# A convolution and score kernel: third products one pair late at the end, low parts on GpSimd, channel 62 averaged on TensorE, last output in four pieces

## The reference

```python
# layer 0: a long convolution per channel, by FFT of twice the size; k is the outer product of two filters
k = einsum('ijk,imk->ijmk', hx, hy)[0]                 # hx, hy: small sine networks times a decay
z = irfft2(rfft2(x) * rfft2(k) / 512)[..., :256, :256] + x * bias
# layer 1, per channel, all 4 images
scores = einsum('bpsd,bptd->bpst', z, z) / sqrt(256)
red = sum(scores * weights[None], axis=-1, keepdims=True)
y = z + red
out = (y - mean(y)) * rsqrt(var(y) + 1e-5) * gamma + beta   # mean and var over images, rows and columns
```

## Time and profile before

| what | value |
|---|---|
| median of 3 runs | 959.41 us (957.51, 959.53, 959.41) |
| profiled execution, own time | 957.47 us |
| its span, first to last instruction | 955.0 us |
| PE busy | 932.5 us, 98% |
| DVE, ACT, GpSimd busy | 751.8, 682.0, 668.0 us |
| mean granted clock of PE | 0.990 |

### The profile page before, as it was taken

How to read it: one execution, slowest core, us unless ns; L and a number is a source line. 1 busy time by engine, 2 the same in 40 slices (tenths; PEclk the granted TensorE clock), 3 DMA queues, 4 the chain that set the end, 5 groups by cost and what they waited for, 6 DMA issues and landing times.

```text
span 955.0 us, 18894 instructions
## 1 busy us (share of the span) xinstructions
PE 932.5 (98%) x5308; PEld 816.1 (85%) x5308; DVE 751.8 (79%) x2460; ACT 682.0 (71%) x1088; POOL 668.0 (70%) x518
## 2 busy tenths in 40 slices
PE   7999999999999999999999999999999999999993
PEld 5888888888888888888888888888888888888882
DVE  2677887887887888878878878878788788788785
ACT  2447777777777777777777777777777777777756
POOL 2676776777777767767767767777777677677650
PEclk9999999999999999999999999999999999999996
DMA  7767998888899998888798999988898899888735
GB/s 224 262 177 214 252 259 293 266 239 289 241 266 297 233 292 278 287 233 273 243 276 283 223 303 272 290 260 246 258 274 267 291 211 304 289 274 244 245 121 182
DMA packets 91439, 244.23 MB, mean 256 GB/s; under 512 B 17312, under 2 KB 42272, under 8 KB 83232
## 3 DMA queue, kind: packets, MB, share of 16 engines
q1 hardware_dynamic: 73280, 235.73, 82.5%
q10 hardware_dynamic: 18144, 8.33, 3.5%
HBM read 176.65 MB, written 67.37 MB: 256 GB/s over the span
## 4 chain that ended last, share of the span: by engine, by line
PE 95%; issue 2%; DVE 1%; DMA 1%; POOL 1%; ACT 0%; POOLq 0%; DVEq 0%
PE ps_c L507 36%; PE ps_u L507 31%; PE ps_z L507 27%; DMA toep_whole<-filters_padded 1%; DVE z_sb L680 0%; DMA par<-params_in 0%; POOL zl L402 0%; DVE products L702 0%; DMA filters_padded<-z_sb 0%; DVE z_sb L786 0%; DVE z_sb L614 0%; POOL toep L376 0%; DVE ul L729 0%; POOL rstd L364 0%; ACT zh L491 0%
## 5 line engine op out<-in xcount | busy, mean ns | idle before, releaser
L402 POOL TENSOR_TENSOR zl<-z_sb,zh 128x1024 fp32r<-128x1024 f32 x126 | 301.5, 2393 | 237.3 <-ACT zh L491 237.3
L702 DVE CUSTOM_DVE_ANT_0 products<-z_sb,ps_c 128x256 bf16<-128x256 f32 x508 | 183.7, 418 | 155.2 <-PE ps_c L507 155.2
L507 PE MATMUL ps_z<-uh,toep 128*128 128x512 f32 x768 | 271.4, 408 | 0.1
L469 ACT ACTIVATE out_sb<-z_sb,shift,gain 128x256 f32<-128x256 f32 x496 | 257.2, 591 | 11.6 <-DMA out<-out_sb 6.1
L448 ACT ACTIVATE uh<-ps_u 128x1024 fp32r<-128x1024 f32 x127 | 130.5, 1027 | 177.7 <-PE ps_u L507 177.7
L507 PE MATMUL ps_u<-toep,xh 128*128 128x256 f32 x1016 | 235.5, 313 | 2.8 <-POOL toep L376 2.7
L507 PE MATMUL ps_c<-zh,wh 128*128 128x512 f32 x508 | 197.8, 389 | 1.2 <-DVE zl L691 0.7
L507 PE MATMUL ps_c<-zh,wl 128*128 128x512 f32 x508 | 197.7, 389 | 0.0
L507 PE MATMUL ps_c<-zl,wh 128*128 128x512 f32 x508 | 197.7, 389 | 0.0
L507 PE MATMUL ps_u<-toep_whole,xt_sb 128*128 128x128 f32 x1016 | 196.0, 274 | 0.0
L713 DVE BATCH_NORM_STATS2 stat<-z_sb 128x6 f32<-128x256 f32 x512 | 179.4, 413 | 0.0
(11 more groups left out here) (72 smaller groups left out, 907.0 us busy)
## 6 DMA issues: line engine op xcount, KB each, us to landing
xt_sb<-xt_in SPq DMA_DIRECT2D x64, 1024.0 KB, 10.3
x_sb<-x_in SPq DMA_DIRECT2D x128, 512.0 KB, 8.4
out<-out_sb SPq DMA_DIRECT2D x124, 512.0 KB, 6.8
w_sb<-wt_in SPq DMA_DIRECT2D x64, 256.0 KB, 7.2
toep_whole<-filters_padded SPq DMA_DIRECT2D x64, 256.0 KB, 7.4
everyone<-partition_moments ACTq DMA_DIRECT2D x63, 128.0 KB, 8.8
out<-z_sb SPq DMA_DIRECT2D x4, 512.0 KB, 2.8
partition_moments<-own ACTq DMA_DIRECT2D x63, 1.0 KB, 5.7
```

Of the source, the lines that this page charges most:

```text
L402: nc.gpsimd.tensor_tensor(zl[:, zs.slot(2)], z_sb[:, r, h], zh[:, zs.slot(2)].bitcast(F32), ALU.subtract)\
L469: last = nc.scalar.activation(to[:, k, b], z_sb[:, r, h, k, b], ACT.Identity, bias=shift[:, r, g:g + 1], scale=gain[:, r])
L507: return nc.tensor.matmul(o, a, b, start=start, stop=stop)
L702: last = nc.vector.tensor_tensor_reduce(products[:, cs.slot(2), k, b], z_sb[:, r, h, k, b], bank[:, k, b], 1.0 / math.sqrt(SIDE), 0.0, ALU ...
```

## The change

- In steps 128 and 129 PE runs only third product 124, one half (output block) in each; 125, 126 and 127 come in the ending, in `ps_u`, `ps_c`, `ps_u`. DVE sums 124 in step 129.
- `zl` of pairs 126 and 127 is computed by GpSimd. `zh` and `zl` of pair 127 lie in slot 0 of `uh` and `ul` and wait for second product 126 instead of an earlier third product.
- Channel 62's moments are no longer sent through DRAM but averaged by PE, as channel 63's are, between and behind the halves of third product 127. `ps_avg` and `last_moment` get a place for each of the two channels.
- GpSimd's power for channel 61 and shift for channel 62 move behind its `zl(127)`; DVE's ending is reordered.
- Channel 63 is stored in four pieces of 256 KB, each as soon as its block is normed; ACT's two instructions are both in the second half.

```diff
         return st.static() and PAIRS - count <= st.number() < PAIRS
+    def last_pair(st):
+        return st.static() and st.number() == PAIRS - 1
...
+        last_moment = sb("last_moment", [P, 2, 1])
+        ps_avg = ps("ps_avg", [P, 2, 3])
...
             return par[:, bass.ds(st.channel(COL_CHAN + kind * CH), 1)]
+        def z_parts(zs):
+            if last_pair(zs):
+                return uh[:, 0], ul[:, 0]
+            return zh[:, zs.slot(2)], zl[:, zs.slot(2)]
...
                     if ending(done, 2):
-                        sp.wait_ge(last_done, done.number() - (PAIRS - 2) + 1)
-                        sp.wait_ge(last_done_act, done.number() - (PAIRS - 2) + 1)
+                        for k in range(BLOCKS):
+                            sp.wait_ge(last_done, BLOCKS * h + k + 1)
+                            if h == 1:
+                                sp.wait_ge(last_done_act, k + 1)
+                            sp.dma_start(out[m, :, h, k, :, :].rearrange("p b w -> p (b w)"),
+                                         normed[:, k].rearrange("p b w -> p (b w)"))\
+                                .then_inc(stored[h], 16)
...
             for h in range(2):
-                sp.wait_ge(stored[h], 16 * CH)
+                sp.wait_ge(stored[h], 16 * (CH - 1 + BLOCKS))
...
                 ms = st.trail(LAG_MEAN)
-                if starts(ms):
+                if starts(ms) and not ending(ms, 4):
...
                 vs = st.trail(LAG_POWER)
-                if starts(vs) and not ending(vs, 4):
+                if starts(vs) and not ending(vs, 6):
...
                 zs = st.trail(LAG_Z)
-                if active(zs) and not ending(zs, 2):
+                if active(zs):
...
                     r, h = zs.ring(XR), zs.half()
-                    nc.gpsimd.tensor_tensor(zl[:, zs.slot(2)], z_sb[:, r, h],
-                                            zh[:, zs.slot(2)].bitcast(F32), ALU.subtract)\
+                    high, low = z_parts(zs)
+                    nc.gpsimd.tensor_tensor(low, z_sb[:, r, h], high.bitcast(F32), ALU.subtract)\
...
             run_steps(pool, PAIRS, 2 * UNROLL, LAG_MEAN - 3, stage)
+            inverse_deviation(Step(0, PAIRS - 6))
+            shift_means(Step(0, PAIRS - 4))
...
                 ms = st.trail(LAG_MEAN)
-                if starts(ms) and not ending(ms, 2):
+                if starts(ms) and not ending(ms, 4):
...
                 ss = st.trail(LAG_SPREAD)
-                if starts(ss) and not ending(ss, 2):
+                if starts(ss) and not ending(ss, 4):
...
                     wait(act, z_ready, zs, 1)
-                    wait(act, c_done, zs, -1)
+                    if last_pair(zs):
+                        wait(act, y_done, zs, 0)
+                    else:
+                        wait(act, c_done, zs, -1)
                     r, h = zs.ring(XR), zs.half()
-                    nc.scalar.activation(zh[:, zs.slot(2)], z_sb[:, r, h],
-                                         ACT.Copy).then_inc(zh_ready, 1)
+                    nc.scalar.activation(z_parts(zs)[0], z_sb[:, r, h], ACT.Copy).then_inc(zh_ready, 1)
...
             act.wait_ge(last_shift, 1)
-            for i in range(PAIRS - 2, PAIRS):
-                r, h = i // 2 % XR, i % 2
-                rows = z_sb[:, r, h, BLOCKS - 1, PAIR - 1]
-                g = (h * BLOCKS + BLOCKS - 1) * PAIR + PAIR - 1
+            r = (CH - 1) % XR
+            for k in range(BLOCKS):
+                rows = z_sb[:, r, 1, k, PAIR - 1]
+                g = (BLOCKS + k) * PAIR + PAIR - 1
...
                 last.then_inc(y_done, 1)
-            def product_c(cs, bank):
+            def product_c(cs, bank, blocks=range(BLOCKS)):
...
                 wait(pe, zl_ready, cs, 1)
-                s, w = cs.slot(2), cs.ring(2)
-                for a in range(BLOCKS):
+                w = cs.ring(2)
+                high, low = z_parts(cs)
+                for a in blocks:
...
                         w_h, w_l = wh[:, w, k, P * a:P * (a + 1)], wl[:, w, k, P * a:P * (a + 1)]
-                        mm(bank[:, a], w_h, zh[:, s, k], k == 0, False)
-                        mm(bank[:, a], w_h, zl[:, s, k], False, False)
-                        last = mm(bank[:, a], w_l, zh[:, s, k], False, k == BLOCKS - 1)
-                last.then_inc(c_done, 1)
+                        mm(bank[:, a], w_h, high[:, k], k == 0, False)
+                        mm(bank[:, a], w_h, low[:, k], False, False)
+                        last = mm(bank[:, a], w_l, high[:, k], False, k == BLOCKS - 1)
+                if BLOCKS - 1 in blocks:
+                    last.then_inc(c_done, 1)
...
                 cs = st.trail(LAG_RED)
-                if active(cs):
+                if st.static() and st.number() >= PAIRS:
+                    late = Step(0, PAIRS - 4)
+                    wait(pe, red_ready, late, 0)
+                    product_c(late, ps_c, [st.number() - PAIRS])
+                elif active(cs):
...
             run_steps(pe, PAIRS, UNROLL, END_STEPS, stage)
-            end = [Step(0, i) for i in range(PAIRS - 2, PAIRS)]
-            product_y(end[1])
+            end = [Step(0, i) for i in range(PAIRS - 3, PAIRS)]
+            def average_first(m):
+                pe.wait_ge(mean_in, m + 1)
+                mm(ps_avg[:, m % 2, 0:2], ones[:, :].bitcast(F32), own[:, m % XR], True, True).then_inc(averaged, 1)
+            def average_moment(m):
+                pe.wait_ge(moment_in, m - (CH - 2) + 1)
+                mm(ps_avg[:, m % 2, 2:3], ones[:, :].bitcast(F32), last_moment[:, m % 2], True, True)\
+                    .then_inc(averaged, 1)
+            product_y(end[2])
+            product_c(end[0], ps_u)
+            pe.wait_ge(red_ready, PAIRS - 3)
+            product_c(end[1], ps_c)
             pe.wait_ge(red_ready, PAIRS - 2)
-            product_c(end[0], ps_c)
-            product_c(end[1], ps_u)
-            pe.wait_ge(mean_in, CH)
-            mm(ps_avg[:, 0:2], ones[:, :].bitcast(F32), own[:, (CH - 1) % XR], True, True).then_inc(averaged, 1)
-            pe.wait_ge(moment_in, 1)
-            mm(ps_avg[:, 2:3], ones[:, :].bitcast(F32), last_moment[:, :], True, True).then_inc(averaged, 1)
+            product_c(end[2], ps_u, [0])
+            average_first(CH - 2)
+            product_c(end[2], ps_u, [1])
+            average_moment(CH - 2)
+            average_first(CH - 1)
+            average_moment(CH - 1)
...
                     op0=ALU.mult, op1=ALU.add).then_inc(z_ready, 1)
-            def low_z(zs):
-                nc.vector.tensor_tensor(zl[:, zs.slot(2)], z_sb[:, zs.ring(XR), zs.half()],
-                                        zh[:, zs.slot(2)].bitcast(F32), ALU.subtract)\
-                    .then_inc(zl_ready, 1)
...
                 cs = st.trail(LAG_RED)
-                if active(cs):
+                if st.static() and st.number() >= PAIRS:
+                    if st.number() == PAIRS + 1:
+                        gain_and_offset(Step(0, PAIRS - 8))
+                        reduce_rows(Step(0, PAIRS - 4), ps_c)
+                elif active(cs):
...
             run_steps(dve, PAIRS, 2 * UNROLL, END_STEPS, stage)
-            end = [Step(0, i) for i in range(PAIRS - 2, PAIRS)]
+            end = [Step(0, i) for i in range(PAIRS - 3, PAIRS)]
             before, final = Step(0, PAIRS - 4), Step(0, PAIRS - 2)
-            low_z(end[0])
-            whole_z(end[1])
+            def first_averages(vs):
+                r, e = vs.ring(XR), vs.ring(2)
+                dve.wait_ge(averaged, 2 * e + 1)
+                nc.vector.tensor_scalar(neg_mean[:, r], ps_avg[:, e, 0:1], -1.0, None, ALU.mult)\
+                    .then_inc(neg_mean_ready, 1)
+                nc.vector.tensor_scalar(var_sum[:, e], ps_avg[:, e, 1:2], BN_EPS, None, ALU.add)\
+                    .then_inc(var_sum_ready, 1)
+                dve.wait_ge(neg_mean_ready, vs.channel(1))
+                nc.vector.tensor_scalar(dev[:, r], own[:, r, 0:1], neg_mean[:, r], None, ALU.add)\
+                    .then_inc(dev_ready, 1)
+                dve.wait_ge(dev_ready, e + 1)
+                nc.vector.tensor_scalar(last_moment[:, e], dev[:, r], dev[:, r], None, ALU.mult)\
+                    .then_inc(moment_in, 1)
+            def second_average(vs):
+                r, e = vs.ring(XR), vs.ring(2)
+                dve.wait_ge(averaged, 2 * e + 2)
+                dve.wait_ge(var_sum_ready, vs.channel(1))
+                nc.vector.tensor_scalar(veps[:, r], ps_avg[:, e, 2:3], var_sum[:, e], None, ALU.add)\
+                    .then_inc(veps_ready, 1)
+            whole_z(end[2])
+            statistics(end[1])
             totals(Step(0, PAIRS - 6))
-            gain_and_offset(Step(0, PAIRS - 8))
+            reduce_rows(end[0], ps_u)
+            gain_and_offset(Step(0, PAIRS - 6))
             mean_of_partition(before)
-            statistics(end[0])
-            low_z(end[1])
-            reduce_rows(end[0], ps_c)
```

(36 more changed lines are left out.)

## The result

The changed kernel took 954.81 us in the median of 11 runs (952.06 to 956.86), the kernel before 959.41 in 11 (956.32 to 961.53). The ratio is 0.9945, 95% interval 0.9931 to 0.9959. The gain of the medians is 4.60 us. The forecast was 952.9 us, from a gain of 5.75 us. The control further down, in another session, gave 0.9931 (0.9917 to 0.9946): 951.94 against 958.56 us, a gain of 6.62.

A forecast was written before the change was run, and what follows sets the result against it. TensorE is busy 98% of the span, but ScalarE's norms of channel 62 set the end; moving them from 949.27 to 943.5 with an unchanged tail gains 5.75 us. Forecast 952.9 us, between 951.7 and 953.7; range 950.9 to 955.8.

The forecast's parts named there:

- 5.73 us from 943.5: Time from the end of ScalarE's norms of channel 62 to the span's end, forecast unchanged at 5.73 us.
- two supposed levels: Runs of the kernel before read as two levels 2 us apart; forecast set between 951.7 and 953.7 us.
- Part 1: TensorE's order: third product 124 cut into halves, first product 127 forward by 1.36 us, third product 125 covering a wait.
- The new wait: TensorE before second product 127, waiting for z(126) to leave bank ps_z: 0.4 us.
- Part 2: Low parts on GpSimd, 2.39 us each, hidden by 0.3 us; VectorE waits 0.7 us for the power behind them.
- Rival C: GpSimd becomes the bound if the norm of pair 120 waits for a free out_sb: 1.3 us, 954.2; chance 0.08.
- Part 3: Channel 62's averages on TensorE instead of through DRAM: two short matmuls inside 1.15 us of slack, cost 0.
- Part 4: Channel 63's output stored in four pieces of 262 KB: taken at 0 us, queue never running dry.
- the 350: Sign of being wrong: the last output's pieces running under 350 GB/s or apart.
- the upper bound: Last stores at 234 GB/s, so 1.05 MB takes 4.5 instead of 2.6 us: +1.9 us.
- Rival B: Tail pays for the pieces: +1.9 us by slow rows or +3.0 by fixed parts, time 955.4; chance 0.09.
- Rival D: The 0.4 us wait and cut sequence drop TensorE's clock to 1.2 GHz: 2.0 us slower than before, 960.6; chance 0.03.

The follow-up runs named there:

- The control further down: The changed kernel itself, unedited, rerun in a third session beside the kernel before: 951.94 us, ratio 0.9931.
- e4: Changed kernel with third products 124 and 125 back whole in steps 128 and 129: ratio to the kernel before 0.9957, ending 33.65 us.
- e2: Changed kernel with the low parts of pairs 126 and 127 back on VectorE: ratio to the kernel before 0.9939, ending 32.02 us.
- e3: Changed kernel with channel 62's moments sent through DRAM again, transfers in ScalarE's queue: ratio to the kernel before 0.9986, ending 36.43 us.
- e5: Kernel before with one line moved, gain and offset of channel 60 ahead of the low part of pair 126: ratio 0.9983, ending 36.36 us.
- e1: Changed kernel with channel 63 stored in two pieces instead of four: ratio to the kernel before 0.9937, ending 31.72 us.
- e10: Changed kernel with four output buffers instead of two, beside the unedited changed kernel: 951.92 us against 951.94, ratio to the kernel before 0.9932.
- e7: Changed kernel with pair 125 normed on VectorE and ScalarE taking three of the last eight norms: ratio to the kernel before 0.9911, ending 30.61 us.
- e11: Changed kernel with four output buffers, shared norm, useless matmuls and pair 124 stored in two pieces: 949.21 us, ratio to the kernel before 0.9901.

## Why the prediction was right

**The direction, the mechanism and the size held**; the step that was mis-sized is the tail, "5.73 us from 943.5". By the ending the forecast was 31.41 us (949.25 - 917.84), measured 31.89. The median lies 1.9 us above the 952.9 forecast: 0.76 us came in by taking the mean of two supposed levels, 0.48 is the ending, and 0.67 lies outside it, where the kernels scatter by more than that.

**Part 1.** Worth 2.2 us by norm 62 (e4). z(127) was forecast 9.56 us after z(125) and came at 9.60. The new wait was 0.22 us, not 0.4.

**Part 2.** GpSimd hid the low parts from PE, and the power behind zl(127) did hold DVE, 0.72 us for a forecast of 0.7. Undone it is 0.6 us (e2). The sums of 127 end at 20.56 us for a forecast of 20.71. Rival C asked for a wait in ACT's norm of pair 120 and none came.

**Part 3.** Costed as zero on PE, which the chain confirms, but the text never priced its removal. It is the largest part: 5.0 us by norm 62 (e3). These prices are not to be added (2.2 + 0.6 + 5.0 is more than the 5.9 us by which norm 62 moved): each part was undone with the others left in, so each shows what it is worth beside them. e5 shows it from the other end: with the DRAM path left in, halving PE's hole was worth 0.8 us.

**Part 4.** Taken at 0 us; the bytes did flow without a gap, at 373 to 418 GB/s in most windows of half a microsecond where before had 401. One window has 340, under the 350 that the prediction named as a sign of being wrong. The pieces cost 0.1 to 0.2 us by e1 to e4, far from the 1.9 of the upper bound. So the pieces, made to save time, cost some: they could gain nothing while pair 125's store kept the DMA full. What the Trainium skill says against small transfers ("DMA: Bandwidth & Descriptors", Rules for kernel authors) holds in sign only: by its fixed part the prediction had an estimated 4 us, and the trace shows that part overlapped. The rule warns of transfers under 64 KB, and these are of 256 KB.

**What the sum lacked** is 0.3 to 0.5 us that go with a code fetch among the last stores. Norm 62 itself came at 25.50 us for 25.66 forecast; tail 6.39 for 5.73. Rival B had the tail pay 1.9 to 3.0 us for the pieces: right in sign, but about a tenth of that was theirs.

**Rival D.** PE's clock stayed full through the 0.22 us wait; it fell only while PE was idle for 3.14 us before channel 63's first average (windows of the changed kernel):

```profile
936.00:937.00 1.00, 1.00 (x6) 0.56 (x5) 0.96 (x7) 1.00 (x3) 0.00 (x0) 1.00 0.00 0
...
940.00:940.50 0.50, 0.15 (x1) 0.15 (x1) 0.30 (x3) 0.43 (x2) 0.00 (x0) 0.79 0.98 393
940.50:941.00 0.50, 0.44 (x2) 0.35 (x2) 0.03 (x1) 0.50 (x2) 0.00 (x0) 0.50 1.04 418
```

The same idle time doesn't always do it. In e4, and in e10 too, the first average behind it still ran at full clock, 0.38 us instead of 0.58. e4:

```profile
940.30 0.38 PE L525 MATMUL ps_avg<-own,ones 128*128 128x2 f32 x2 [3.14 <-DVE own L703]
```

**The two levels** that the forecast averaged are no levels: 11 runs fill 956.3 to 961.5 us. The profile's own 957.47 is low in that range.

## What to carry to other kernels

Rewrite each engine's queue of a serial ending by hand, with durations from the trace: here 25 us of it came out within 0.2 us. Then price what each part hides, not only what it costs: the largest gain was a path of two small transfers that no hole of the busiest engine pointed at. While the stores run without a gap, the first byte's time and the number of bytes set the end. Splitting the last ones gained nothing here; starting the first ones sooner did (e7), until the norms behind them could not keep the DMA full (e11).

## What was not expected of the hardware

Code is fetched by the same 16 DMA engines as the data: the DMA view counts it among them, as queue 14. A fetch of some 0.01 MB, 0.4 us of one engine, among the last 1.57 MB of stores goes with a trickle of 25 to 30 GB/s at their end and a tail 0.3 to 0.5 us longer.
